# Linear recurrence kernel: one scan over all tiles and both sums, with carry columns, and a new order of the forward loop

## The chip, the cores and the metric

The program runs on one core of a Trainium2 chip. The metric is the device time of one execution in microseconds; before the change it was 7432.79 us (median of 3 runs, 7431.01 to 7443.61).

## The reference, cut to what matters

Two layers on an image tensor of 4 x 192 x 128 x 128 in fp32. The first (channel attention with depthwise convolutions, seven stages of the program) isn't touched by the change. The second is a recurrence in two directions over the 16384 positions of each image, with 192 channels:

```
def step(carry, kv_t):
    p, q, o = carry
    no = jnp.maximum(o, u + kt)
    A = jnp.exp(o - no)
    Bw = jnp.exp(u + kt - no)
    y = (A * p + Bw * vt) / (A * q + Bw)
    no2 = jnp.maximum(w + o, kt)
    A2 = jnp.exp(w + o - no2)
    B2 = jnp.exp(kt - no2)
    return ((A2 * p + B2 * vt, A2 * q + B2, no2), y)
...
x_bi = 0.5 * (x_fwd + x_bwd)
h = jax.nn.sigmoid(r) * x_bi
h = (h - mu) * jax.lax.rsqrt(var + LN_EPS) * ln_g + ln_b
out = jnp.einsum('btc,dc->btd', h, Wo)
```

k, v and r are 192 x 192 projections of the normalised input; mu and var are taken over the channels. The layer's input is added to its output.

## The kernel before, in words

**Stages.** The program is a row of stages that begin and end with a barrier of all engines. The last four are wkv_backward and wkv_forward for images 0 and 1, then again for images 2 and 3. The change touches these two functions and their callers' scratch tensors, nothing else.

**Tiles and chunks.** The 384 channels of two images lie in three tiles of 128 partitions. Positions are cut into 32 chunks of CH = 512. A loop (wkv_steps, line 1231) calls step(n) for n from 0 to 37 on every engine: six steps are written out, then a hardware loop of two steps a round, then six more. In step n an engine works on chunk n, n-1, n-2 or further back, and has(n, lag) leaves out what doesn't exist. There is no scheduler: each engine's work stands in the order in which step lists it, the engines run in order, and semaphores named x_done couple them (a wait for x_done of n-1 waits for chunk n-2, since counts begin at one).

**Backward stage, a chunk.** PE forms k (tile pk) and v (tile pv) by project (lines 1204 to 1210, seven products). v's bias comes from three products of a row of ones with the row vrow (line 1348), which open pv's sums. DVE takes k's maximum (line 1418), ACT forms b = exp(k - max) (bl, line 1369), DVE b v (bvl, line 1442); both are stored to HBM for the forward stage. ACT scales both by a per-channel factor (bf, line 1380; bvf, line 1385), and DVE scans each: three scans of 512 for q (qq, called at line 1473) and three for p (pp). The first column of each scan is the carry, a product of the last chunk's end and a factor (lines 1467 and 1468). Then den = bf eu + q (line 1447) and num = bvf eu + p (line 1455), ACT takes 1/den as exp(-ln den) (lines 1390, 1392), and DVE forms y (yb, line 1432).

**Forward stage, a chunk.** b and b v are read back and scaled (lines 1659, 1664), scanned (line 1800) and made into den and num (lines 1753, 1762) as before. PE forms r (pr); ACT forms exp(-r) (sg, line 1669), DVE clamps it (line 1746), and ACT makes the sigmoid in two more passes (1678, 1680). DVE forms num/den (rc, line 1773), adds the backward y (line 1777) and multiplies by the sigmoid: h (hh, line 1781). The norm over channels needs two averages on PE: of h (pm) and of h squared (pq; ACT's squares are hsq, line 1642), both by average (lines 1598 to 1600). From pm and pq come msq, var (line 1769), lv and rs (lines 1683 to 1689); DVE scales h by rs (hn_done, line 1784). PE then forms the output in po: three products with the identity that bring in the residual xr (line 1620), and project with Wo. ACT writes po to xo (ev_done, line 1695), and SP stores it.

```
if has(n, 2):
    pe.wait_ge(h_done, n - 1)
    average(pm, hh[:, h]).then_inc(mean_done, 1)
if has(n):
    wait(pe, er_done, n)
    project(nc, pr, wr, xt[:, h]).then_inc(r_done, 1)
if has(n, 2):
    pe.wait_ge(hsq_done, n - 1)
    average(pq, hsq).then_inc(st_done, 1)
if has(n, 3):
    for tile in range(3):
        mm(po[:, tile, :], ident[:, :], xr[:, g, tile, :], start=True, stop=False, skip_group_check=True)
    pe.wait_ge(hn_done, n - 2)
    project(nc, po, wo, hh[:, g], begin=False).then_inc(o_done, 1)
```

Of the kernel before, what the change touches and what calls it, by code (L numbers as in the profile page):

```python
# [19 lines left out]
ALU = mybir.AluOpType  # L20
# [1222 lines left out]
def wkv_backward(nc, pair, x1, stat1, wkt, wvt, decay, bonus, b_d, bv_d, y_d, mx_d):  # L1243


    with Stage(nc, f"wb{pair}") as st:
# [6 lines left out]
        vrow = st.sb("vrow", [1, 3, 128])  # L1253
        ones = st.sb("ones", [1, CH])
        xt = st.sb("xt", [128, 2, 3, CH])
        bl = st.sb("bl", [128, 2, 3, CH])
        bvl = st.sb("bvl", [128, 2, 3, CH])
        bf = st.sb("bf", [128, 2, 3, CH])
        bvf = st.sb("bvf", [128, 2, 3, CH])
        qq = st.sb("qq", [128, 2, 3, CH + 1])  # L1260
        pp = st.sb("pp", [128, 2, 3, CH + 1])
        den = st.sb("den", [128, 3, CH])
        num = st.sb("num", [128, 2, 3, CH])
# [15 lines left out]
        bv_stored = [st.sem(f"bv_stored{h}") for h in range(2)]  # L1279
        y_stored = [st.sem(f"y_stored{h}") for h in range(2)]  # L1280
        (k_done, v_done, maxed, m_done, s_max, d_done, b_done, f_done, bf_done, bv_done, bvf_done, carried, q_done,
         scanned, den_done, num_done, ln_done, rc_done, y_done, mx_stored) = map(
            st.sem, ("k_done", "v_done", "maxed", "m_done", "s_max", "d_done", "b_done", "f_done", "bf_done", "bv_done",
                     "bvf_done", "carried", "q_done", "scanned", "den_done", "num_done", "ln_done", "rc_done", "y_done",
                     "mx_stored"))
        block = st.block()

        def chunk(n):
            return NCH - 1 - n

        @block.sync
        def _(sp):
# [7 lines left out]
            def step(n, h, t):  # L1300
# [585 lines left out]
```

## Time and profile before

| | |
|---|---|
| median of 3 runs | 7432.79 us |
| the profiled execution | 7438.61 us |
| its span, first to last instruction | 7435.9 us |
| PE busy | 5760.8 us (77%) |
| DVE busy | 5662.4 us (76%) |
| ACT busy | 2748.5 us (37%) |
| first backward stage, its chunks | from 4816 us on |
| last instruction of DVE in the second forward stage | 7418 us |

PE is TensorE, DVE VectorE, ACT ScalarE, POOL GpSimd, SP the queue that issues most DMAs. Busy time counts an engine's instructions; PEclk or the granted clock is TensorE's clock as a share of full speed. A row of the timeline gives start, duration, engine, line, operation, tiles and how many instructions were merged; brackets hold the idle time before it and what ended it.

### The profile page before, as it was taken

How to read it: one execution, taken by the hardware profiler on the slowest of the kernel's cores; microseconds unless marked ns; L12 is line 12 of the kernel's file. 1: busy time of each engine (PE TensorE's matmuls, PEld its weight loads, DVE VectorE, ACT ScalarE, POOL GpSimd, SP SyncE). 2: the span in 40 equal slices, each digit the busy share in tenths (PEclk: the TensorE clock that was granted, in tenths of full speed). 3: DMA queues.
4: the chain of work that ended last, by engine and by line, in shares of the span. 5: the costliest groups of instructions: out<-in, count | busy, mean ns of one | idle time of the engine just before them, and what ended most of it. 6: DMA issues, size and time to landing. Idle time of an engine off the chain costs nothing. (4 is left out here: it accounts for less than half of the span.)

```text
span 7435.9 us, 82986 instructions
## 1 busy us (share of the span) xinstructions
PE 5760.8 (77%) x25278; PEld 2354.1 (32%) x25278; DVE 5662.4 (76%) x5546; ACT 2748.5 (37%) x3703; POOL 341.1 (5%) x539
## 2 busy tenths in 40 slices
PE   0999997799899566455565777699768879985888
PEld 0333332333333465233332222232222223222222
DVE  6333332799999777888885666599979978997998
ACT  0222221111111466111110000055479974556998
POOL 0110100000000000122220000000000000000000
PEclk9999998899999787777777788787779988787999
DMA  7556554999999997899997999754456644445665
GB/s 292 174 177 198 182 190 152 221 270 274 270 275 277 235 230 179 209 247 255 248 249 181 267 270 267 189 186 183 164 198 230 231 164 170 183 178 182 231 230 181
DMA packets 1209065, 1615.58 MB, mean 217 GB/s; under 512 B 87604, under 2 KB 907509, under 8 KB 1195509
## 3 DMA queue, kind: packets, MB, share of 16 engines
q1 hardware_dynamic: 1067125, 1419.06, 65.6%
q10 hardware_dynamic: 115200, 100.71, 5.1%
q0 software_dynamic: 26624, 94.40, 5.1%
q8 instruction: 57, 0.93, 0.1%
q14 instruction: 59, 0.48, 0.0%
HBM read 1006.55 MB, written 607.33 MB: 217 GB/s over the span
## 5 line engine op out<-in xcount | busy, mean ns | idle before, releaser
L501 PE MATMUL dw_p<-dw_it,dw_tt 128*128 128x512 f32 x2304 | 1027.1, 607 | 177.0 <-DMA dw_it<-u 176.3
L541 DVE SCALAR_TENSOR_TENSOR dw_vo<-dw_vi,dw_wv,dw_vo 128x2048 f32<-128x2048 f32 x384 | 903.1, 2352 | 13.6
L836 PE MATMUL bc_p<-bc_z,bc_wc 128*32 128x256 f32 x9216 | 572.8, 414 | 399.4 <-DVE bc_z L875 399.4
L289 PE MATMUL pw_p<-pw_xh,pw_wlo 128*112 128x512 f32 x1536 | 693.2, 601 | 184.4 <-POOL pw_xh L263 184.4
L875 DVE STREAM_TRANSPOSE bc_z<-bc_xp 128x1536 f32<-128x1536 f32 x256 | 711.8, 2850 | 154.1 <-DMA bc_xp<-d 153.7
L1084 PE MATMUL ap_p<-ap_vt,ap_pw 96*96 96x512 f32 x1024 | 584.3, 736 | 186.5 <-DMA ap_xt<-in_x 184.7
L501 PEld LDWEIGHTS dw_p<-dw_it,dw_tt 128*128 128x128 f32 x2304 | 441.7, 193 | 762.5 <-issue 745.4
L516 ACT ACTIVATE dw_ot<-dw_p 128x512 f32<-128x512 f32 x384 | 206.7, 608 | 997.3 <-DMA d<-dw_ot 703.6
L344 DVE COPY pw_ut<-pw_p 112x512 f32<-112x512 f32 x384 | 247.3, 685 | 379.5 <-PE pw_p L295 377.5
L836 PEld LDWEIGHTS bc_p<-bc_z,bc_wc 128*32 128x32 f32 x9216 | 323.8, 119 | 648.5 <-issue 487.2
L814 ACT ACTIVATE bc_xt<-bc_p 128x256 f32<-128x256 f32 x384 | 147.4, 384 | 874.7 <-PE bc_p L836 874.7
L289 PEld LDWEIGHTS pw_p<-pw_xh,pw_wlo 128*112 128x112 f32 x1536 | 261.8, 177 | 608.2 <-issue 534.1
L658 DVE TENSOR_REDUCE gr_ss<-gr_sq 128x24 f32<-128x3072 f32 x64 | 320.8, 5080 | 127.1 <-ACT gr_sq L642 126.8
L1117 DVE TENSOR_TENSOR ap_xo<-ap_p,ap_tt 96x512 f32<-96x512 f32 x256 | 172.9, 685 | 283.1 <-PE ap_p L1084 166.6
L619 PE MATMUL gr_p<-gr_qk 128*48 128x48 f32 x4096 | 290.5, 337 | 123.1 <-DMA gr_qk<-d 87.8
L1084 PEld LDWEIGHTS ap_p<-ap_vt,ap_pw 96*96 96x96 f32 x1024 | 200.5, 202 | 570.1 <-issue 533.9
L642 ACT ACTIVATE gr_sq<-gr_qk 128x3072 f32<-128x3072 f32 x64 | 319.4, 5061 | 159.0 <-DMA gr_qk<-d 120.2
L295 PE MATMUL pw_p<-pw_xh,pw_whi 64*112 64x512 f32 x1536 | 362.6, 604 | 0.0
L619 PEld LDWEIGHTS gr_p<-gr_qk 128*48 128x48 f32 x4096 | 288.4, 239 | 127.2 <-issue 118.8
L339 DVE COPY pw_ut<-pw_p 16x512 f32<-16x512 f32 x128 | 83.7, 692 | 298.4 <-PE pw_p L295 298.4
L321 ACT ACTIVATE pw_ut<-pw_p 112x512 f32<-112x512 f32 x256 | 138.7, 594 | 423.3 <-PE pw_p L295 423.3
L1167 ACT ACT_TABLE_LOAD x1 | 1.3, 1283 | 767.5 <-issue 767.5
(310 smaller groups left out, 9845.4 us busy)
## 6 DMA issues: line engine op xcount, KB each, us to landing
u<-pw_ut SPq DMA_DIRECT2D x64, 2240.0 KB, 12.6
dw_it<-u SPq DMA_DIRECT2D x192, 512.0 KB, 7.2
d<-dw_ot SPq DMA_DIRECT2D x192, 512.0 KB, 7.3
gr_qk<-d SPq DMA_DIRECT2D x128, 768.0 KB, 9.0
bc_xp<-d SPq DMA_DIRECT2D x256, 288.0 KB, 12.0
bc_xp<-d POOLq DMA_DIRECT2D x256, 288.0 KB, 9.9
gs_xt<-in_x SPq DMA_DIRECT2D x24, 2048.0 KB, 7.2
d<-dw_vo SPq DMA_DIRECT2D x96, 512.0 KB, 7.8
```

The costliest lines, as they stand in the source:

```text
L289: mm(pt[m % NBANK][e][:, :], wlo[:, wm], xh[:, h, 2 * e, cols], start=True, stop=False, skip_group_check=True)
L295: last = mm(pt[m % NBANK][e][:, :], whi[p, wm], xh[p, h, 1, cols], start=False, stop=True, skip_group_check=True)
L344: last = nc.vector.tensor_copy(rows_back(0, h, e, m, q), by_row(pt[m % NBANK][e][:, :]))
L501: mm = nc.tensor.matmul(po[c][:, :].rearrange("p (b w) -> p b w", b=B), tt[:, h, 3 * c + dx, 0:H], it[:, h, B * c:B * (c + 1), dx:dx + W], ...
L516: nc.scalar.activation(ot[:, h, c, :], po[c][:, :], ACT.Copy).then_inc(by_act, 1)
L541: nc.vector.scalar_tensor_tensor(vo[:, h], src, w, vo[:, h], ALU.mult, ALU.add).then_inc(tapped, 1)
L619: mm = nc.tensor.matmul(pg[h][p:p + CPG, :], qk[:, h, 0:CPG, w], qk[:, h, CPG:QK, w], start=w < 2, stop=w >= W - 2, skip_group_check=True)
L642: nc.scalar.activation(sq[:, e % 2, :, :].rearrange("p c w -> p (c w)"), qk[:, h, E * e:E * e + E, :].rearrange("p c w -> p (c w)"), ACT.S ...
L658: nc.vector.tensor_reduce(ss[:, n % 2, E * e:E * e + E], sq[:, e % 2, :, :], AX.X, ALU.add).then_inc(reduced, 1)
L836: mm = nc.tensor.matmul(po[q % NBANK][32 * c4:32 * c4 + 32, :, :], wc[:, c, dx, :, :].rearrange("p j r -> p (j r)"), z[:, h, c, :, dx:dx + ...
L875: last = nc.vector.transpose(z[:, h, :, b % 2, 1 + S * k:1 + S * k + S], xp[:, b % 2, k, :, :].rearrange("p s c -> p c s"))
L1084: mm = nc.tensor.matmul(po[2 * q + m][:, :], pw[:, b, k, m * HALF:(m + 1) * HALF], vt[:, b % 2, k, q * SUB:(q + 1) * SUB], start=k == 0, s ...
```

## The change

- b and b v share one tile (bb), their scaled forms another (fb), with one more column for each tile and sum. The carry is written into that column in one operation, the decay is spread into a tile ewt whose carry columns are 0, and one scan of 6 x 513 = 3078 columns takes the place of six of 512.
- den and num become one tile dn, made by three operations of 2 x 512 columns in place of six of 512. ACT scales b and b v by three operations of 2 x 512 in place of six of 512. b and b v are stored and loaded by one DMA in place of two.
- v's bias is no longer added by PE. It is kept as a column vb (twice the bias) and added where h is formed: the one addition of 1536 columns in the forward stage becomes three of 512 with a scalar operand.
- The order inside step changes, in the forward stage on PE, ACT and DVE: ln and exp of den, the products r and the evictions move by one chunk.

PE, the end of one step and the beginning of the next in the forward loop (wf_po the output, wf_pm and wf_pq the averages of h and of h squared, wf_pr the product r). Before:

```order
L1210 MATMUL wf_po<-wf_hh,wf_wo 64x512
...
L1598 MATMUL wf_pm<-wf_hh,wf_oneb 128x512
L1599 MATMUL wf_pm<-wf_hh,wf_one 64x512
L1600 MATMUL wf_pm<-wf_hh,wf_one 64x512
...
L1204 MATMUL wf_pr<-wf_xt,wf_wr 128x512
...
L1210 MATMUL wf_pr<-wf_xt,wf_wr 64x512
L1598 MATMUL wf_pq<-wf_hsq,wf_oneb 128x512
...
L1620 MATMUL wf_po<-wf_xr,wf_ident 128x512 x3
```

And with the change:

```order
L1586 MATMUL wf_po<-wf_xr,wf_ident 128x512 x3
...
L1572 MATMUL wf_pm<-wf_hh,wf_oneb 128x512
L1573 MATMUL wf_pm<-wf_hh,wf_one 64x512
L1574 MATMUL wf_pm<-wf_hh,wf_one 64x512
L1204 MATMUL wf_po<-wf_hh,wf_wo 128x512
...
L1210 MATMUL wf_po<-wf_hh,wf_wo 64x512
L1572 MATMUL wf_pq<-wf_hsq,wf_oneb 128x512
L1573 MATMUL wf_pq<-wf_hsq,wf_one 64x512
L1574 MATMUL wf_pq<-wf_hsq,wf_one 64x512
...
L1204 MATMUL wf_pr<-wf_xt,wf_wr 128x512
```

Before, r stood right behind pm and ahead of pq, and po ended the step. Now the step runs r, the identity products, pm, po, pq, and the next step's r stands behind pq.

ACT, one step of the same loop. Before:

```order
L1642 ACTIVATE wf_hsq<-wf_hh 128x1536
...
L1648 ACTIVATE wf_fac<-wf_diff 128x6
L1653 ACTIVATE wf_msq<-wf_pm 128x512
L1659 ACTIVATE wf_bf<-wf_bl,wf_fac 128x512 x3
L1664 ACTIVATE wf_bvf<-wf_bvl,wf_fac 128x512 x3
L1669 ACTIVATE wf_sg<-wf_pr,wf_nrb 128x512 x3
L1674 ACTIVATE wf_rc<-wf_den 128x1536
L1676 ACTIVATE wf_rc<-wf_rc 128x1536
L1678 ACTIVATE wf_sg<-wf_sg,wf_onev 128x1536
```

And with the change:

```order
L1617 ACTIVATE wf_rc<-wf_dn 128x1536
L1619 ACTIVATE wf_rc<-wf_rc 128x1536
L1624 ACTIVATE wf_xo<-wf_po,wf_cb 128x512 x3
L1630 ACTIVATE wf_sg<-wf_pr,wf_nrb 128x512 x3
...
L1636 ACTIVATE wf_fac<-wf_diff 128x6
L1642 ACTIVATE wf_fb<-wf_bb,wf_fac 128x2x512 x3
L1647 ACTIVATE wf_lv<-wf_var,wf_eps 128x512
L1650 ACTIVATE wf_rs<-wf_lv 128x512
L1653 ACTIVATE wf_rs<-wf_lv 64x512 x4
L1657 ACTIVATE wf_sg<-wf_sg,wf_onev 128x1536
L1659 ACTIVATE wf_sg<-wf_sg 128x1536
L1663 ACTIVATE wf_hsq<-wf_hh 128x1536
```

Before, the exponential that reads r stood behind the scalings of b and b v; now it stands ahead of the scaling, and the squares, which opened the step, stand near its end.

The diff, cut to its core (mostly the new lines):

```diff
+def spread_decay(nc, dve, ewt, ew, slot, spread):
+
+    for tile in range(3):
+        last = nc.vector.tensor_copy(ewt[:, tile].rearrange("p b t -> p (b t)"), ew[:, tile, :].to_broadcast([128, 2 * CH + 2]))
+    last.then_inc(spread, 1)
+    dve.wait_ge(spread, 1)
+    nc.vector.memset(ewt[:, :, :, slot:slot + 1], 0.0).then_inc(spread, 1)
+    dve.wait_ge(spread, 2)
+
+
+def carry(nc, dve, m, slots, ends, factor, scanned, carried):
+
+    if isinstance(m, int) and m == 0:
+        nc.vector.memset(slots, 0.0).then_inc(carried, 1)
+    else:
+        dve.wait_ge(scanned, m)
+        nc.vector.tensor_tensor(slots, ends, factor.rearrange("p (t a) -> p t a", a=1).to_broadcast([128, 3, 2]),
+                                ALU.mult).then_inc(carried, 1)
+    dve.wait_ge(carried, m + 1)
...
@@ wkv_backward, PE, ACT, DVE
-                for tile in range(3):
-                    mm(pv[:, tile, :], vrow[:, tile, :], ones[:, :], start=True, stop=False, skip_group_check=True)
-                project(nc, pv, wv, xt[:, h], begin=False).then_inc(v_done, 1)
+                project(nc, pv, wv, xt[:, h]).then_inc(v_done, 1)
...
+                    act.wait_ge(bv_done, n + 1)
+                    wait(act, dn_done, n - 1)
                     for tile in range(3):
...
+                        last = nc.scalar.activation(fb[:, h, tile, :, 0:CH], bb[:, h, tile, :, :], ACT.Copy,
+                                                    scale=fac[:, h, 1, tile:tile + 1])
+                    last.then_inc(fb_done, 1)
...
+                if has(n, 1):
+                    dve.wait_ge(f_done, n)
+                    dve.wait_ge(fb_done, n)
+                    carry(nc, dve, n - 1, fb[:, g, :, :, CH], sums[:, :, :, 0], fac[:, g, 0, :], scanned, carried)
+                    wait(dve, dn_done, n - 1)
+                    nc.vector.tensor_tensor_scan(row(sums[:, :, :, :])[:, ::-1], row(ewt[:, :, :, :])[:, ::-1], row(fb[:, g])[:, ::-1],
+                                                 ewt[:, 2, 1, CH:CH + 1], ALU.mult, ALU.add).then_inc(scanned, 1)
                 if has(n, 2):
...
+                    nc.vector.tensor_tensor(yb[:, h], dn[:, :, 1, :], rc[:, :, :], ALU.mult).then_inc(y_done, 1)
...
@@ wkv_forward, PE
+                if has(n, 1):
+                    pe.wait_ge(x_loaded[g], 64 * (t + h))
+                    wait(pe, er_done, n - 1)
+                    project(nc, pr, wr, xt[:, g]).then_inc(r_done, 1)
                 if has(n, 3):
...
                     for tile in range(3):
                         mm(po[:, tile, :], ident[:, :], xr[:, g, tile, :], start=True, stop=False, skip_group_check=True)
+                if has(n, 2):
+                    pe.wait_ge(h_done, n - 1)
+                    wait(pe, msq_done, n - 2)
+                    average(pm, hh[:, h]).then_inc(mean_done, 1)
+                if has(n, 3):
                     pe.wait_ge(hn_done, n - 2)
                     project(nc, po, wo, hh[:, g], begin=False).then_inc(o_done, 1)
+                if has(n, 2):
+                    pe.wait_ge(hsq_done, n - 1)
+                    wait(pe, var_done, n - 2)
+                    average(pq, hsq).then_inc(st_done, 1)
...
@@ wkv_forward, ACT
+                    act.wait_ge(dn_done, n - 1)
...
+                if has(n, 1):
+                    act.wait_ge(r_done, n)
+                    wait(act, h_done, n - 2)
+                    for tile in range(3):
+                        last = nc.scalar.activation(sg[:, g, tile, :], pr[:, tile, :], ACT.Exp, bias=nrb[:, tile:tile + 1], scale=-1.0)
+                    last.then_inc(er_done, 1)
...
@@ wkv_forward, DVE
                 if has(n, 1):
+                    dve.wait_ge(f_done, n)
+                    dve.wait_ge(fb_done, n)
+                    carry(nc, dve, n - 1, fb[:, g, :, :, 0], sums[:, :, :, CH], fac[:, g, 0, :], scanned, carried)
+                    wait(dve, dn_done, n - 1)
+                    nc.vector.tensor_tensor_scan(row(sums[:, :, :, :]), row(ewt[:, :, :, :]), row(fb[:, g]), ewt[:, 0, 0, 0:1],
+                                                 ALU.mult, ALU.add).then_inc(scanned, 1)
+                if has(n, 3):
...
+                    nc.vector.tensor_tensor(var[:, :], pq[:, :], msq[:, :], ALU.subtract).then_inc(var_done, 1)
+                if has(n, 1):
                     dve.wait_ge(er_done, n)
                     nc.vector.tensor_scalar(flat(sg[:, g]), flat(sg[:, g]), 2.0 ** 60, None, ALU.min).then_inc(cl_done, 1)
...
+                if has(n, 2):
+                    dve.wait_ge(rc_done, n - 1)
+                    nc.vector.tensor_tensor(rc[:, :, :], dn[:, :, 1, :], rc[:, :, :], ALU.mult).then_inc(yf_done, 1)
+                    dve.wait_ge(yf_done, n - 1)
+                    dve.wait_ge(y_loaded[h], 16 * t)
+                    for tile in range(3):
+                        last = nc.vector.scalar_tensor_tensor(rc[:, tile, :], rc[:, tile, :], vb[:, tile:tile + 1],
+                                                              yb[:, h, tile, :], ALU.add, ALU.add)
+                    last.then_inc(hs_done, 1)
...
+                    nc.vector.tensor_tensor(flat(hh[:, h]), flat(rc[:, :, :]), flat(sg[:, h]), ALU.mult).then_inc(h_done, 1)
+                if has(n, 3):
+                    dve.wait_ge(rs_done, n - 2)
+                    nc.vector.tensor_tensor(flat(hh[:, g]), flat(hh[:, g]), flat(rs[:, :, :]), ALU.mult).then_inc(hn_done, 1)
+                if has(n, 1):
+                    dve.wait_ge(scanned, n)
                     wait(dve, ln_done, n - 1)
+                    wait(dve, yf_done, n - 1)
                     for tile in range(3):
...
+                        last = nc.vector.scalar_tensor_tensor(dn[:, tile], fb[:, g, tile, :, 1:CH + 1], eu[:, tile, :],
+                                                              sums[:, tile, :, 0:CH], ALU.mult, ALU.add)
+                    last.then_inc(dn_done, 1)
```

## Rows read from the trace of the kernel before

**Rows 1.** Stretches: length, busy PE, PEld, DVE, ACT, POOL, PEclk, DMA share, GB/s

```profile
6800.00:7340.00 540.00, 476.59 (x1214) 148.56 (x1212) 529.57 (x606) 496.49 (x657) 0.00 (x0) 0.92 0.66 226
6200.00:6660.00 460.00, 425.42 (x916) 135.55 (x915) 453.86 (x567) 236.22 (x323) 0.00 (x0) 0.81 0.49 184
```

**Rows 2.** Timeline of DVE, one step of the backward loop (start us, us)

```profile
6300.35 3.64 DVE L1473 TENSOR_TENSOR_SCAN wb_qq<-wb_ew,wb_qq,wb_bf 128x512 f32<-128x512 f32 x3
...
6307.54 3.63 DVE L1473 TENSOR_TENSOR_SCAN wb_pp<-wb_ew,wb_pp,wb_bvf 128x512 f32<-128x512 f32 x3
6311.20 2.08 DVE L1455 SCALAR_TENSOR_TENSOR wb_num<-wb_bvf,wb_eu,wb_pp 128x512 f32<-128x512 f32 x3
...
6317.20 0.16 DVE L1467 TENSOR_TENSOR wb_qq<-wb_qq,wb_fac 128x3 f32<-128x3 f32 x1
...
6317.47 3.64 DVE L1473 TENSOR_TENSOR_SCAN wb_qq<-wb_ew,wb_qq,wb_bf 128x512 f32<-128x512 f32 x3
```

**Rows 3.** Groups of instructions by line: busy us, mean ns of one, idle before

```profile
L1473 DVE TENSOR_TENSOR_SCAN wb_pp<-wb_ew,wb_pp,wb_bvf 128x512 f32<-128x512 f32 x192 | 232.2, 1265 | 0.0
L1455 DVE SCALAR_TENSOR_TENSOR wb_num<-wb_bvf,wb_eu,wb_pp 128x512 f32<-128x512 f32 x192 | 132.9, 747 | 4.7
L1390 ACT ACTIVATE wb_rc<-wb_den 128x1536 f32<-128x1536 f32 x64 | 94.9, 1483 | 23.1 <-DVE wb_den L1447 20.9
```

**Rows 4.** Waits of DVE over the whole execution, and the bias products of a step

```profile
DVE wb_bvl L1442 <- PE wb_pv L1210: 18.5, 4, 6.9
...
6305.69 3.66 PE L1348 MATMUL wb_pv<-wb_ones,wb_vrow 1*128 1x512 f32 x6 [0.68 <-DVE wb_bvl L1442]
```

**Rows 5.** Timeline of DVE and ACT, one step of the forward loop

```profile
6998.89 3.63 DVE L1800 TENSOR_TENSOR_SCAN wf_qq<-wf_ew,wf_qq,wf_bf 128x512 f32<-128x512 f32 x3
...
7004.56 1.84 ACT L1669 ACTIVATE wf_sg<-wf_pr,wf_nrb 128x512 f32<-128x512 f32 x3 [1.42 <-PE wf_pr L1210]
...
7010.81 1.75 DVE L1773 TENSOR_TENSOR wf_rc<-wf_num,wf_rc 128x1536 f32<-128x1536 f32 x1
7012.77 1.76 DVE L1777 TENSOR_TENSOR wf_num<-wf_rc,wf_yb 128x1536 f32<-128x1536 f32 x1 [0.21 <-DVE wf_rc L1773]
7014.56 1.76 DVE L1781 TENSOR_TENSOR wf_hh<-wf_num,wf_sg 128x1536 f32<-128x1536 f32 x1
...
7016.46 1.12 PE L1598 MATMUL wf_pm<-wf_hh,wf_oneb 128*128 128x512 f32 x2 [2.46 <-DVE wf_hh L1781]
...
7018.34 0.95 DVE L1746 TENSOR_SCALAR wf_sg<-wf_sg 128x1536 f32<-128x1536 f32 x1
...
7019.47 1.28 DVE L1800 TENSOR_TENSOR_SCAN wf_qq<-wf_ew,wf_qq,wf_bf 128x512 f32<-128x512 f32 x1
```

**Rows 6.** Timeline of PE in the forward loop: pq, identity, po, and pm

```profile
7066.01 1.13 PE L1598 MATMUL wf_pq<-wf_hsq,wf_oneb 128*128 128x512 f32 x2
...
7068.08 2.84 PE L1620 MATMUL wf_po<-wf_xr,wf_ident 128*128 128x512 f32 x6
7070.76 1.02 PE L1204 MATMUL wf_po<-wf_hh,wf_wo 128*128 128x512 f32 x2
...
7074.97 0.59 PE L1210 MATMUL wf_po<-wf_hh,wf_wo 128*64 128x512 f32 x1
```

**Rows 7.** Timeline of PE after two longer idle times, and TensorE's clock by stretch

```profile
7405.88 2.07 PE L1598 MATMUL wf_pm<-wf_hh,wf_oneb 128*128 128x512 f32 x2 [6.75 <-DVE wf_hh L1781]
...
7409.79 1.25 PE L1598 MATMUL wf_pq<-wf_hsq,wf_oneb 128*128 128x512 f32 x2
...
5468.59 2.07 PE L1598 MATMUL wf_pm<-wf_hh,wf_oneb 128*128 128x512 f32 x2 [8.15 <-DVE wf_hh L1781]
...
5472.50 2.08 PE L1204 MATMUL wf_pr<-wf_xt,wf_wr 128*128 128x512 f32 x2
5474.37 1.20 PE L1205 MATMUL wf_pr<-wf_xt,wf_wr 128*128 128x512 f32 x2
...
7058.60:7062.10 3.50, 3.50 (x7) 1.10 (x7) 3.34 (x9) 3.28 (x6) 0.00 (x0) 0.53 0.86 280
```

More of the change, by code:

```diff
@@ L1445, in step @@
                     wait(dve, ln_done, n - 1)
+                    wait(dve, y_done, n - 1)
                     for tile in range(3):
-                        last = nc.vector.scalar_tensor_tensor(den[:, tile, :], bf[:, g, tile, :], eu[:, tile, :],
-                                                              qq[:, g, tile, 1:CH + 1], ALU.mult, ALU.add)
-                    last.then_inc(den_done, 1)
-                    dve.wait_ge(bvf_done, n)
-                    scans(g, pp, bvf).then_inc(scanned, 1)
@@ L1471, in scans @@
[L1471 to L1476 removed]
+                        last = nc.vector.scalar_tensor_tensor(dn[:, tile], fb[:, g, tile, :, 0:CH], eu[:, tile, :],
+                                                              sums[:, tile, :, 1:CH + 1], ALU.mult, ALU.add)
@@ L1671, in step @@
[L1671 to L1676 removed]
+                        last = nc.scalar.activation(fb[:, h, tile, :, 1:CH + 1], bb[:, h, tile, :, :], ACT.Copy,
+                                                    scale=fac[:, h, 1, tile:tile + 1])
@@ new lines, in step @@
+                    last.then_inc(fb_done, 1)
+                if has(n, 3):
+                    act.wait_ge(var_done, n - 2)
+                    nc.scalar.activation(lv[:, :], var[:, :], ACT.Ln, bias=eps[:, 0:1]).then_inc(lv_done, 1)
+                    act.wait_ge(lv_done, n - 2)
+                    wait(act, hn_done, n - 3)
+                    nc.scalar.activation(rs[:, 1, :], lv[:, :], ACT.Exp, scale=-0.5)
+                    for tile, lo in ((0, 0), (2, 64)):
+                        for p in (0, 64):
+                            last = nc.scalar.activation(rs[p:p + 64, tile, :], lv[lo:lo + 64, :], ACT.Exp, scale=-0.5)
+                    last.then_inc(rs_done, 1)
@@ L1755, in step @@
-                    last.then_inc(den_done, 1)
-                if has(n, 1):
-                    dve.wait_ge(bvf_done, n)
-                    scans(g, pp, bvf).then_inc(scanned, 1)
-                    dve.wait_ge(scanned, n)
-                    wait(dve, hs_done, n - 1)
-                    for tile in range(3):
-                        last = nc.vector.scalar_tensor_tensor(num[:, tile, :], bvf[:, g, tile, :], eu[:, tile, :],
-                                                              pp[:, g, tile, 0:CH], ALU.mult, ALU.add)
-                    last.then_inc(num_done, 1)
@@ L1798, in scans @@
-            def scans(h, sums, term):
-                for tile in range(3):
-                    last = nc.vector.tensor_tensor_scan(sums[:, h, tile, 1:CH + 1], ew[:, tile, :].to_broadcast([128, CH]),
-                                                        term[:, h, tile, :], sums[:, h, tile, 0:1], ALU.mult, ALU.add)
-                return last
+                        last = nc.vector.scalar_tensor_tensor(dn[:, tile], fb[:, g, tile, :, 1:CH + 1], eu[:, tile, :],
+                                                              sums[:, tile, :, 0:CH], ALU.mult, ALU.add)
```

291 lines of the change are left out of this document (83 added, 208 removed).

## The prediction

> **What bounds the kernel now.** The change touches only the last four stages, so I began with the busy time by stretch [rows 1]. In the forward loop DVE is busy for 529.57 of 540 us (98%) and ACT for 496.49 (92%), in the backward loop DVE for 453.86 of 460 (99%) and ACT for 51%. So today both loops go at the pace of DVE, and ACT has 8% to spare in the forward one. Then the timelines: the same scan returns after 17.12 us backward (6300.35 to 6317.47) [rows 2] and after 20.58 us forward (6998.89 to 7019.47) [rows 5]. That is one step, one chunk. There are 32 chunks in each of two backward and two forward stages.
>
> A DVE that is full says only that shorter DVE work may help; whether it does depends on what the new order makes of the loop. So I then followed, engine by engine, what each operation stands behind and what it waits for.
>
> **The change, part by part: DVE's work.** Three scans last 3.63 us and one alone 1.265, so they follow each other by (3.63 - 1.265)/2 = 1.18 us for 512 columns [rows 2, 3]. The trace has only this one length. If nothing of it were fixed, 3078 columns would take 3078/512 x 1.265 = 7.6 us; if a column cost only what it costs the addition of 1536 (1.76 us, so 1.15 ns) [rows 5], 3.5 us. The nearest row for the fixed part is the other three-operand operation, three of which last 2.08 and one 0.747, so 0.67 apart [rows 2, 3]: about 0.12 us fixed. With that a scanned column costs (1.18 - 0.12)/512 = 2.07 ns and the long scan 6.5 us. I take 6.5 and keep 3.5 and 7.6.
>
> By the Trainium skill's page DVE: opcode table, instruction layouts, handler registers and perf-mode slots (section Datapath and trigger behaviour) the scan "runs at half throughput"; that would be 6.4 us as an estimate, and no row here separates it from the fixed part.
>
> Before, a step held 3.54 + 3.66 us of scans (a scan with a waiting successor goes 3.66, 6307.54 to 6311.20 [rows 2]). Now 6.53: saved 0.67. The six operations for den and num took 6 x 0.67 = 4.02; three of 1024 columns take 3 x (2 x 0.67 - 0.12) = 3.66: saved 0.36. Two carry products become one: 0.27 (6317.20 to 6317.47 [rows 2]) becomes 0.19, saved 0.08. **Backward, a step: 1.11 us less**, 17.12 to 16.01. I looked for what could take DVE's place there: ACT's work falls from 51% of a step, PE loses the three bias products (3.66 us a step [rows 4]), and the scan of chunk n-1, which now waits for both scaled tiles, has den and num of the chunk before and the next maximum between them and itself (3.7 + 1.8 us, while ACT's whole work of a step is 236.22/460 x 17.12 = 8.8 us, of which the scaling is a part [rows 1]). So it stays with DVE: 32 x 1.11 = 35.5 us. At its start a backward stage waits for v (18.5 us in 4 waits over both stages [rows 4]); two of these get shorter by the 3.66 us of bias products, 7 us a stage. At its end, ln and exp of the last den (2 x 1.483 us [rows 3]) no longer lie beside a scan: 3 us back. About 39.5 us a stage, **79 us less for both**. The tile ewt I cost at nothing, since DVE fills it while the weights are loaded; without that cover its three copies of 1026 columns would cost some 2 us a stage (the clamp takes 0.95 us for 1536 [rows 5]).
>
> The VectorE page (VectorE: DVE Perf Modes, section on the TRN2 errata) gives a fixed part of only 58 cycles, 0.06 us, for an operation. By it the nine operations fewer would save 0.54 us a step, not 1.11, and the total would be 36 us higher. The rows show about 0.12, and the sum goes by them.
>
> **The forward order.** DVE's own work there falls by 0.67 + 0.36 + 0.08, and the addition with the bias, three operations (2.08) and a wait in place of 1.79 (7012.77 to 7014.56 [rows 5]), gives back 0.34: 19.8 us against 20.58. But PE's and ACT's new orders close a ring. PE now runs r of the next chunk behind pq; pq stands behind po, po behind pm; pm waits for h. h needs DVE's sums, DVE comes to them only after the clamp, and the clamp waits for ACT's exponential of r, in the same step. So every step holds, one behind the other: r; exponential; clamp; num/den; sum; h; pm; po; pq; and then the next r. Before, r stood behind pm, and neither po nor pq lay between h and r; DVE didn't reach h through r of the same step alone.
>
> The ring's price, from start to start: r, seven products like po's, which run from 7070.76 to 7074.97 + 0.59, 4.80 us [rows 6]; exponential 1.84 and two hops of 0.05 [rows 5]; clamp 0.86 (0.95 less an overlap of 0.09); num/den 1.96 (7010.81 to 7012.77); the three additions 2.13; h until pm starts 1.90 (7014.56 to 7016.46) [rows 5]; pm, po, pq. At full clock pm is like pq, 2.07 (7066.01 to 7068.08), and po 4.80 [rows 6]. Sum: 4.80 + 1.94 + 0.86 + 1.96 + 2.13 + 1.90 + 2.07 + 4.80 + 2.07 = **22.5 us**. That is more than the 20.58 of today before anything else is counted.
>
> Then the clock. In the ring PE stands idle from the end of the identity products (2.68 us behind r [rows 6]) to h: 1.94 + 0.86 + 1.96 + 2.13 + 1.90 - 2.68 = 6.1 us, in every step. Today it is idle for 2.46 us there [rows 5], and even so its clock drops to 0.53 for the next 3.5 us, the 1.2 GHz level [rows 7]. After 6.75 us of idle, pm took 3.91 us and what followed ran at full speed but for 0.1; after 8.15 us pm took 3.91, and the next two products 1.87 and 1.04 where they take 0.85 and 0.86, 1.2 us more [rows 7]. So pm costs 1.84 more and po 0.1 to 1.2 more; I take 0.7. **A forward step: 25.1 us**, between 24.5 and 25.6, against 20.58: 4.5 us more. The ring is closed in 30 of a stage's steps (po begins with step 3 and r ends with step 32), and at the end pq of the last chunk stands behind one more po, 5 us: 30 x 4.5 + 5 = 140 us a stage, **280 us more for both**.
>
> The transfers I cost at nothing: b and b v are one DMA of the same bytes, SP waits for nothing later than before, and DMA's share is 0.66 forward and 0.49 backward [rows 1].
>
> **The sum.** 7438.6 (the profiled execution) - 79 + 280 = 7639.6. That execution lies 5.8 us above the median of 7432.8, so I forecast **7634 us** for the median, slower by 2.7%.
>
> **The rivals.**
> (a) The ring isn't closed: some wait is met earlier than I read it and DVE still sets the pace, as its 98% today suggests [rows 1]. Then a forward step takes 19.8, 50 us less for both stages, and with the backward 79 less: 7433 - 129 = 7304 us. For it speaks that ACT already waits for r today (1.42 us [rows 5]) without harm. Against it speaks the order of the rows. It decides at one number: the kernel gets faster only if a forward step stays under 20.58 + (79 - 10)/60 = 21.7 us.
> (b) The ring is closed but PE keeps its full clock: 22.5 us a step, 2 x (30 x 1.9 + 5) = 124 more, 79 less: 7478 us. Against it, each of the idle rows [rows 7]. The page TensorE: Matmul & The Clock Gate (Part 1) says that for modeling the ramp is under 1% of a typical span; the difference between (b) and my forecast is 2.1%, so by that rule (b) would be it.
> (c) The long scan costs 7.6 us. The forward ring hides it, since the scan isn't in it; the backward gain falls by 64 x 1.07 = 68: 7702 us. If it costs 3.5, the backward stages gain 192 more: 7442 us, no change. The fixed parts speak against both.
>
> **How the numbers follow.** About 0.2%, 15 us, is what a measurement can tell from no change. My forecast 0.74, (a) 0.13, (b) 0.07, (c) dear 0.04, (c) cheap 0.02. Slower by more than 0.2%: 0.74 + 0.07 + 0.04 = 0.85, less 0.01 for a ring and clock that both come out short, 0.84; faster: (a) and half of the cheap scan, 0.14; the same 0.02. The range: a step of 24.5 gives 36 us less, and a backward gain larger by 20 another 20 less: 7578. It reaches down towards (b), to 7540, since the clock is the least certain term; upwards a step of 25.6 gives 30 more, with part of the dear scan 7710. Left out are (a), (b) and the cheap scan.
>
> **What would show it.** In the changed profile: a forward loop with DVE busy near 80%, a wait of DVE's clamp on ACT's exponential of r of some 5 us a step, PE idle for about 6 us ahead of pm and pm at half clock in every step, and a step of 25 us. In the backward loop one scan of 3078 columns of 6.6 us, DVE still busy to 98%, a step of 16.0 us. I am wrong if DVE is busy to 95% and more in the forward loop, or if PE shows no idle time ahead of pm.

## The result and the profile after

| | before | after |
|---|---|---|
| median | 7435.3 us (4 runs, 7431.0 to 7443.6) | 7571.5 us (4 runs, 7565.4 to 7575.9) |
| profiled span | 7435.9 us | 7563.8 us |
| PE busy | 77% | 5523.5 us (73%) |
| DVE busy | 76% | 5564.5 us (74%) |

The kernel became slower: the ratio is 1.0174, with a 95% interval of 1.0159 to 1.0188, so about 136 us by the medians. (One execution of e6 below, 8987.6 us at a granted clock of 0.60, was a slow one and isn't in its row.) The forecast was 7634 us, and the range 7540 to 7710. The direction and the mechanism came out as forecast; the size was 201 us in the forecast and 136 in the runs.

The busy time of the changed kernel by stretch (us; then busy time and instructions of PE, PEld, DVE, ACT, POOL; granted clock; DMA share; GB/s), a forward and a backward stretch, to be put beside [rows 1]:

```profile
6880.00:7420.00 540.00, 410.18 (x1016) 122.87 (x1018) 430.60 (x355) 410.20 (x490) 0.00 (x0) 0.85 0.58 194
6280.00:6680.00 400.00, 284.57 (x703) 89.38 (x702) 396.15 (x302) 200.64 (x225) 0.00 (x0) 0.90 0.51 195
```

Backward, DVE is still the bound (99% busy). Forward, it is busy for 430.60 of 540 us, 80%, where it was busy to 98%, and no other engine took its place: PE and ACT are both at 76%. So it is waits between the engines that set the step. The groups say for whom:

```profile
L1720 DVE TENSOR_TENSOR_SCAN wf_sums<-wf_ewt,wf_fb 128x3078 f32<-128x3078 f32 x64 | 424.3, 6630 | 2.3
L1751 DVE SCALAR_TENSOR_TENSOR wf_dn<-wf_fb,wf_eu,wf_sums 128x1024 f32<-128x1024 f32 x192 | 234.9, 1278 | 0.0
L1729 DVE TENSOR_SCALAR wf_sg<-wf_sg 128x1536 f32<-128x1536 f32 x64 | 61.3, 959 | 250.1 <-ACT wf_sg L1630 250.1
L1630 ACT ACTIVATE wf_sg<-wf_pr,wf_nrb 128x512 f32<-128x512 f32 x192 | 118.1, 686 | 300.4 <-PE wf_pr L1210 300.4
L1572 PE MATMUL wf_pm<-wf_hh,wf_oneb 128*128 128x512 f32 x128 | 132.3, 1137 | 384.2 <-DVE wf_hh L1742 384.2
```

The last three rows are the ring: the clamp waits 250.1 us for ACT's exponential, that exponential 300.4 us for r, and pm, over the 64 chunks of both stages, 384.2 us (6.0 a chunk, 5.7 to 5.9 in the steady steps) for h. Before, that wait was 198.7 us in all, and 2.4 to 2.5 a step in the steady part. One step of it in the timeline (start, duration, engine, line, operation, idle time before and its releaser), rows of all three engines:

```profile
7149.82 2.07 PE L1572 MATMUL wf_pm<-wf_hh,wf_oneb 128*128 128x512 f32 x2 [5.74 <-DVE wf_hh L1742]
7153.73 1.57 PE L1204 MATMUL wf_po<-wf_hh,wf_wo 128*128 128x512 f32 x2
7159.01 1.13 PE L1572 MATMUL wf_pq<-wf_hsq,wf_oneb 128*128 128x512 f32 x2
7161.08 1.13 PE L1204 MATMUL wf_pr<-wf_xt,wf_wr 128*128 128x512 f32 x2
7166.04 1.84 ACT L1630 ACTIVATE wf_sg<-wf_pr,wf_nrb 128x512 f32<-128x512 f32 x3 [4.98 <-PE wf_pr L1210]
7167.91 0.96 DVE L1729 TENSOR_SCALAR wf_sg<-wf_sg 128x1536 f32<-128x1536 f32 x1 [4.44 <-ACT wf_sg L1630]
7168.79 1.75 DVE L1732 TENSOR_TENSOR wf_rc<-wf_dn,wf_rc 128x1536 f32<-128x1536 f32 x1
7170.67 2.08 DVE L1736 SCALAR_TENSOR_TENSOR wf_rc<-wf_rc,wf_vb,wf_yb 128x512 f32<-128x512 f32 x3
7172.78 1.76 DVE L1742 TENSOR_TENSOR wf_hh<-wf_rc,wf_sg 128x1536 f32<-128x1536 f32 x1
7174.67 2.07 PE L1572 MATMUL wf_pm<-wf_hh,wf_oneb 128*128 128x512 f32 x2 [5.90 <-DVE wf_hh L1742]
7178.57 1.13 PE L1204 MATMUL wf_po<-wf_hh,wf_wo 128*128 128x512 f32 x2
```

Each row is the first of a group that starts when the group above it is done (pm has six products, po and r fourteen): 24.85 us from pm to pm. pm takes 3.91 us both times (7149.82 to 7153.73), and the granted clock in it is 0.50, the 1.2 GHz level; from 7160 to 7165, with PE busy throughout, it is 1.00:

```profile
7149.80:7153.50 3.70, 3.68 (x6) 0.79 (x6) 3.15 (x3) 3.64 (x4) 0.00 (x0) 0.50 0.62 219
7160.00:7165.00 5.00, 5.00 (x17) 1.65 (x18) 3.48 (x2) 1.06 (x2) 0.00 (x0) 1.00 0.82 256
```

The backward step, answering to [rows 2], is one scan and 15.86 us from scan to scan (the steps alternate between 15.85 and 15.95, where they were 17.1):

```profile
6354.27 6.63 DVE L1436 TENSOR_TENSOR_SCAN wb_sums<-wb_ewt,wb_fb 128x3078 f32<-128x3078 f32 x1
...
6370.13 6.63 DVE L1436 TENSOR_TENSOR_SCAN wb_sums<-wb_ewt,wb_fb 128x3078 f32<-128x3078 f32 x1
```

**The account.** From the first to the last start of the operation that forms h, a forward stage takes 745.2 us both times (the second from 6786.23 to 7531.39) where it took 636.4 and 635.7: 108.8 and 109.5 more, 218 for both. From the first to the last negated maximum, a backward stage takes 484.7 where it took 528.1 and 526.3: 43.4 and 41.6 less, 85 for both. The remaining parts at the ends of the stages add some 6. These four stages together are 139 us longer. The stages ahead of them, which the change doesn't touch, were 11 us shorter in this execution (the first loop starts 4811.7 us into the span with after and 4824.7 with before; the other 2 us of this difference lie in the first backward stage's own start and are counted in the 139; such starts lay between 4799 and 4843 in the runs below). 139 - 11 = 128 is the difference of the spans. Because the untouched part wanders like this, the experiments below are compared by step lengths as well as by times.

### The profile page after: what moved, and what is told of

Its sections match the earlier page's. It is cut to its first block and busy times, and to the rows that moved or that the text cites. A ratio compares the mean times of both kernels' runs of the same rounds, so it can differ in the third digit from the quotient of the medians.

```text
span 7563.8 us, 80038 instructions
## 1 busy us (share of the span) xinstructions
PE 5523.5 (73%) x24890; PEld 2270.0 (30%) x24890; DVE 5564.5 (74%) x4534; ACT 2683.1 (35%) x3319; POOL 342.1 (5%) x539
## 5 line engine op out<-in xcount | busy, mean ns | idle before, releaser
L1436 DVE TENSOR_TENSOR_SCAN wb_sums<-wb_ewt,wb_fb 128x3078 f32<-128x3078 f32 x64 | 424.3, 6630 | 2.3
L1720 DVE TENSOR_TENSOR_SCAN wf_sums<-wf_ewt,wf_fb 128x3078 f32<-128x3078 f32 x64 | 424.3, 6630 | 2.3
L1572 PE MATMUL wf_pm<-wf_hh,wf_oneb 128*128 128x512 f32 x128 | 132.3, 1137 | 384.2 <-DVE wf_hh L1742 384.2
L1389 ACT ACTIVATE wb_fb<-wb_bb,wb_fac 128x1024 f32<-128x1024 f32 x192 | 206.7, 1140 | 475.9 <-DVE wb_bb L1445 475.9
```

The costliest lines, as they stand in the source:

```text
L1436: nc.vector.tensor_tensor_scan(row(sums[:, :, :, :])[:, ::-1], row(ewt[:, :, :, :])[:, ::-1], row(fb[:, g])[:, ::-1], ewt[:, 2, 1, CH:CH + ...
L1720: nc.vector.tensor_tensor_scan(row(sums[:, :, :, :]), row(ewt[:, :, :, :]), row(fb[:, g]), ewt[:, 0, 0, 0:1], ALU.mult, ALU.add).then_inc( ...
```

## The experiments

Unless said otherwise each edit is made on the changed kernel ("after"). The step is the mean distance of h from h in the steady part of the second forward stage. All ratios are to before, with runs of before on the same chip.

| run | ratio to before [95%] | median us | forward step | backward step |
|---|---|---|---|---|
| before | 1 | 7435.3 | 20.5 | 17.1 |
| after | 1.0174 [1.0159, 1.0188] | 7571.5 | 24.4 | 15.9 |
| e1_r_ahead | 0.9800 [0.9784, 0.9817] | 7277.1 | 19.5 | 15.9 |
| e2_pq_behind_r | 1.0154 [1.0137, 1.0171] | 7545.2 | 23.9 | 15.9 |
| e3_filler | 1.0051 [1.0030, 1.0071] | 7469.0 | 22.7 | 15.9 |
| e7_pq_filler | 0.9925 [0.9908, 0.9942] | 7379.6 | 21.3 | 15.9 |
| e4_six_scans | 0.9889 [0.9871, 0.9907] | 7360.7 | 20.0 | 16.4 |
| e5_six_scans_late_r | 1.0223 [1.0202, 1.0245] | 7608.8 | 24.4 | 16.4 |
| e8_order_before | 1.0565 [1.0540, 1.0590] | 7858.4 | 29.0 | 15.9 |
| e10_er_first | 1.0176 [1.0153, 1.0198] | 7561.3 | 23.9 | 15.9 |
| e6_bias_backward (3 runs) | 0.9775 [0.9748, 0.9801] | 7284.6 | 19.3 | 15.9 |

**Is it a ring? (e1_r_ahead)** PE forms r a step earlier, and nothing else changes:

```diff
-                if has(n, 1):
-                    pe.wait_ge(x_loaded[g], 64 * (t + h))
-                    wait(pe, er_done, n - 1)
-                    project(nc, pr, wr, xt[:, g]).then_inc(r_done, 1)
+                if has(n):
+                    pe.wait_ge(x_loaded[h], 64 * (t + 1))
+                    wait(pe, er_done, n)
+                    project(nc, pr, wr, xt[:, h]).then_inc(r_done, 1)
```

> One edit to the changed kernel: in the forward stage PE forms r of chunk n in step n again (before, the change had moved it to chunk n-1), so that ACT's exponential of r finds it ready and r is no longer a link between pq and h. Ring theory: the forward step falls from 24.4 us to DVE's own work, 19.8 us, DVE's wait of the clamp on ACT (250 us over the execution) goes, PE's idle time ahead of pm falls below 3 us; 60 steps x 4.6 us less: about 7290 us, faster than before the change too. Rival (what the forward stage lost is due to the longer work itself, the three additions with the bias and the later var, not to the order of r): the step stays above 22 us and the time above 7430 us.

Measured: 0.9800 of before, step 19.5 us, 294 us under after. The same loop in its timeline and by stretch:

```profile
7001.27 0.95 DVE L1729 TENSOR_SCALAR wf_sg<-wf_sg 128x1536 f32<-128x1536 f32 x1
7007.85 1.12 PE L1572 MATMUL wf_pm<-wf_hh,wf_oneb 128*128 128x512 f32 x2
```

```profile
6700.00:7200.00 500.00, 438.91 (x1175) 138.65 (x1174) 492.56 (x411) 468.86 (x563) 0.00 (x0) 0.96 0.69 239
```

Neither the clamp nor pm has idle time before it any more, pm's first two products take 1.12 us instead of 2.07, and DVE is busy to 99%. One place on PE decided between 7277 and 7572, and with it the changed kernel is faster than the one before.

**How much of the ring is the clock? (e3_filler)** Five products whose result nobody reads go into the wait ahead of pm:

```diff
                 if has(n, 2):
-                    pe.wait_ge(h_done, n - 1)
                     wait(pe, msq_done, n - 2)
+                    for k in range(5):
+                        mm(pm[:, :], oneb[:, :], wr[:, 0:CH], start=True, stop=True, skip_group_check=True)
+                    pe.wait_ge(h_done, n - 1)
                     average(pm, hh[:, h]).then_inc(mean_done, 1)
```

> Work added to the changed kernel and nothing removed: in the forward stage PE runs five more products of 128x512 with constant operands into pm (about 4.3 us) in the idle time ahead of h, overwritten by pm's own. Theory that the half clock behind the idle time is a part of the ring: pm falls from 3.9 us to about 2.1 and the first product of po to its full speed, the step falls by 1.9 us to 22.5 us: about 7455 us, although PE does more. Rival (the clock costs nothing on the path): the time stays at 7571 us; rival (the filler itself delays pm): slower than 7571 us.

```profile
7154.18 1.13 PE L1572 MATMUL wf_pm<-wf_hh,wf_oneb 128*128 128x512 f32 x2 [1.54 <-DVE wf_hh L1744]
7156.43 1.13 PE L1204 MATMUL wf_po<-wf_hh,wf_wo 128*128 128x512 f32 x2
```

```profile
6900.00:7300.00 400.00, 370.16 (x988) 124.10 (x987) 343.97 (x286) 327.33 (x390) 0.00 (x0) 1.00 0.61 208
```

The clock stays at 1.00, pm takes 2.25 us with its last wait (7154.18 to 7156.43) instead of 3.91, the step is 22.67 against the 22.5 worked out for full clock, and the kernel is 102 us faster by the medians for doing more work (91 by the ratios to before; the two forward stages are 105 us shorter from first to last h). So the ring has two parts: about 22.5 us of work behind one another, and 1.9 of lowered clock.

**A shorter ring (e2_pq_behind_r), and the same at full clock (e7_pq_filler).** The second average moves from behind po to behind r; e7 has the filler products of e3 as well:

```diff
+                if has(n, 3):
+                    pe.wait_ge(hsq_done, n - 2)
+                    wait(pe, var_done, n - 3)
+                    average(pq, hsq).then_inc(st_done, 1)
                 if has(n, 3):
                     pe.wait_ge(r_loaded[g], 64 * (t + h - 1))
...
-                if has(n, 2):
-                    pe.wait_ge(hsq_done, n - 1)
-                    wait(pe, var_done, n - 2)
-                    average(pq, hsq).then_inc(st_done, 1)
```

> One edit to the changed kernel: the average of the squares (pq) of chunk n-3 stands behind r of chunk n-1 in the same step instead of ahead of it. Ring theory: pq (2.07 us) leaves the link between po and r, but r now reaches the clamp through pq and var (2.7 us) instead of the exponential (1.94 us), so the ring gets 1.3 us shorter: a step of 23.1 us, about 7490 us. Rival (PE's order is not what binds): no change, 7571 us. Rival (the ring gives back all of pq): 2.07 us a step, 7447 us.

> e2_pq_behind_r (the second average behind r) with the five filler products of e3_filler ahead of the mean; nothing is left out. It asks what ate most of the gain that e2_pq_behind_r was to bring. Theory A (the clock: the step of e2 lost its gain because the stretch of products at half clock got longer): at full clock the shorter ring shows whole, the step is 1.1 to 1.3 us under the 22.67 of e3_filler, so 21.4 to 21.6, and the time about 75 us under e3_filler, near 7395. Theory B (the new wait of VectorE for the second average's variance is the bound in itself): the step stays within 0.4 us of e3_filler's, 22.3 or more, time 7445 or more.

e2 missed its number: 23.9 us a step, 0.5 less than after, where 1.3 was expected. Its timeline shows why (pm, then the first and second pair of po):

```profile
7159.14 2.07 PE L1572 MATMUL wf_pm<-wf_hh,wf_oneb 128*128 128x512 f32 x2 [4.71 <-DVE wf_hh L1742]
...
7163.05 1.88 PE L1204 MATMUL wf_po<-wf_hh,wf_wo 128*128 128x512 f32 x2
7164.76 1.02 PE L1205 MATMUL wf_po<-wf_hh,wf_wo 128*128 128x512 f32 x2
```

po's first pair takes 1.71 us here (7163.05 to 7164.76), and 1.71 and 1.78 in turn over the steps, where at full clock it takes 0.96: pm and po together lose 2.6 us to the clock in each step here, and 2.0 in the mean of after. In e7, at full clock, the same move is worth 1.4 us (22.67 to 21.27), and the time is 7379.6. So the ring did get shorter by about what it should, and 0.6 us of the gain went to the clock (2.6 - 2.0). Most of the 0.3 us that are left lies in e3, whose po waits 0.1 and 0.2 us in turn, in the second case for DVE's product with rs (from pm to po it takes 2.25 and 2.34 us there, against 2.07), which it does not in after. Theory B of e7, a bound in the new wait for the variance, falls.

**What is the merge of the scans worth, and where? (e4_six_scans, e5_six_scans_late_r)** The same edit on e1 and on after:

```diff
-                    nc.vector.tensor_tensor_scan(row(sums[:, :, :, :]), row(ewt[:, :, :, :]), row(fb[:, g]), ewt[:, 0, 0, 0:1],
-                                                 ALU.mult, ALU.add).then_inc(scanned, 1)
+                    for tile in range(3):
+                        for part in range(2):
+                            last = nc.vector.tensor_tensor_scan(sums[:, tile, part, :], ewt[:, tile, part, :],
+                                                                fb[:, g, tile, part, :], ewt[:, 0, 0, 0:1],
+                                                                ALU.mult, ALU.add)
+                    last.then_inc(scanned, 1)
```

> Like e1_r_ahead, but the one scan over 3078 columns is cut into six over 513 columns each (every sum of every tile, each from its own zero decay column), in both stages. Nothing else changes. This prices the merge of the scans by itself, on a kernel in which VectorE is the bound in both stages. Theory (the step of the prediction that took 6.5 us for one scan against the six of before, 1265 ns each behind one another at about 1.2 us): six of 513 columns give a sixth part of 6.63 us each, plus about 0.12 us for each boundary between them, so five boundaries, 0.6 us per step, in 128 steps: +80 us against e1_r_ahead, near 7355. Rival (a fixed part of some 0.06 us per instruction, which the pages state): +0.3 us per step, +40 us, near 7315. Rival (scans behind one another without a dependence overlap): nothing, 7277.

> The changed kernel, order and all, with its one scan over 3078 columns cut into six over 513 in both stages, the same edit that e4_six_scans made on the kernel with r ahead. There it cost 0.55 us per step backward and 0.35 to 0.43 forward. Theory (the forward stage is a ring through PE, ScalarE and VectorE, and the scan lies in front of VectorE's wait for the clamp, outside it): the forward step stays at its 24.3 us mean, the wait ahead of the clamp shrinks from 4.4 by about 0.5, and only the backward stages pay, 16.4 us each: +33 us against the changed kernel, near 7604. Rival (VectorE's own work still counts in the forward stage, since a longer scan pushes the whole step back): +60 us or more, 7632.

With DVE as the bound (e4), six scans last 7.17 us where the one lasts 6.63:

```profile
6313.09 7.17 DVE L1438 TENSOR_TENSOR_SCAN wb_sums<-wb_ewt,wb_fb 128x513 f32<-128x513 f32 x6
```

That is 0.54 us a backward step (15.90 to 16.44), 0.11 per boundary; a forward step gets 0.45 longer (in the mean over both stages), and the time came out at 7360.7, where 7355 was expected. In the ring (e5) the backward step grows by the same 0.54 and the forward step not at all: 743.9 us from first to last h where after has 745.2. The time, 7608.8, is within 5 us of the 7604 that the backward stages alone give. What grows is DVE's work ahead of the clamp, at the expense of its wait, 250.1 us in after and 215.0 here:

```profile
DVE wf_sg L1737 <- ACT wf_sg L1634: 215.0, 60, 5.0
```

So in the changed kernel the long scan of the forward stages gained nothing: what it saved, DVE spent waiting at the clamp.

**Does only r's place matter? (e8_order_before, e10_er_first)** Here TensorE's whole forward order is the one of before, while DVE and ACT keep theirs; e10 exchanges two groups on ACT as well:

```diff
+                if has(n, 2):
...
+                    average(pm, hh[:, h]).then_inc(mean_done, 1)
+                if has(n):
...
+                    project(nc, pr, wr, xt[:, h]).then_inc(r_done, 1)
+                if has(n, 2):
...
+                    average(pq, hsq).then_inc(st_done, 1)
                 if has(n, 3):
...
                     project(nc, po, wo, hh[:, g], begin=False).then_inc(o_done, 1)
```

and on ACT, in e10 alone:

```diff
-                if has(n, 4):
...
-                    last.then_inc(ev_done, 1)
                 if has(n, 1):
                     act.wait_ge(r_done, n)
...
                     last.then_inc(er_done, 1)
+                if has(n, 4):
...
+                    last.then_inc(ev_done, 1)
```

> The changed kernel with TensorE's forward order exactly as in the kernel before (mean of n-2, r of n, second average of n-2, residual and output projection of n-3), while VectorE and ScalarE keep the changed order and the merged operations. Theory (only the place of r matters; the rest of TensorE's order is slack): the same time as e1_r_ahead, within 15 us, forward step near 19.5, near 7277. Rival (the second average now stands ahead of the output projection and holds it until ScalarE's squares come, last in its step, and the next h waits for the projection that reads its slot): forward step 20.5 or more, 7340 or more.

> e8_order_before with two groups of ScalarE's forward step exchanged: the exponentials of r for n-1 now stand ahead of the eviction of the output projection, where they stood behind it. e8_order_before took 28.6 to 29.5 us per step, and its trace shows ScalarE 10 us idle at that eviction, since the projection now comes last on TensorE, with the exponentials queued behind the waiting eviction and the clamp, h and the next mean behind those. Theory (that queue place closes a second ring, through the projection and the eviction): with the exponentials first the ring is open, VectorE's 19.4 to 19.6 us per step are the bound again, ratio to before near 0.98, 7280 to 7300. Rival (the late second average or the projection's slot holds the step in another way): step still over 21 us, 7380 or more.

Both theories of mine were refuted. The times fell on the side of the two rivals (7340 or more, 7380 or more), but the waits aren't the ones that the first of them named. e8 takes 28.6 and 29.5 us a step in turn. ACT in e8, then ACT and DVE in e10:

```profile
7330.09 1.84 ACT L1623 ACTIVATE wf_xo<-wf_po,wf_cb 128x512 f32<-128x512 f32 x3 [9.29 <-PE wf_po L1210]
7331.82 1.85 ACT L1629 ACTIVATE wf_sg<-wf_pr,wf_nrb 128x512 f32<-128x512 f32 x3
```

```profile
7214.60 1.84 ACT L1629 ACTIVATE wf_xo<-wf_po,wf_cb 128x512 f32<-128x512 f32 x3 [4.90 <-PE wf_po L1210]
7216.33 0.21 ACT L1635 ACTIVATE wf_fac<-wf_diff 128x6 f32<-128x6 f32 x1
7216.62 3.23 ACT L1641 ACTIVATE wf_fb<-wf_bb,wf_fac 128x1024 f32<-128x1024 f32 x3
```

```profile
7223.59 1.76 DVE L1744 TENSOR_TENSOR wf_hh<-wf_hh,wf_rs 128x1536 f32<-128x1536 f32 x1 [4.54 <-ACT wf_rs L1652]
```

In e8 the exponential of r has its operand long ago, but stands in ACT's queue behind the eviction of po, which waits 9.29 us for a projection that now comes last on PE. That is a second ring: pm, r, pq, identity products, po, eviction, exponential, clamp, h. In e10 the exponential is ahead, and the step falls from 29.0 to 23.9, which shows that the second ring was the bound of e8. By the trace a third ring takes over, further down the same queue (no run opens this one, so it is read and not tested): behind the waiting eviction (4.90 us) stand fb and rs, DVE's product with rs waits 4.54 us for rs, and den and num, the scan and the next h stand behind that. From this eviction (7214.60) over that h to the pm behind it (7243.39) are 28.8 us, and from the pm before (7195.60) over r, pq, identity products and po to the eviction are 19.0: 47.8 us, which is two steps of 23.9. ACT's order in the changed kernel needs po early on PE. So the changed order of PE is not a mistake as a whole: of the orders run here with ACT's new one, it is the fastest once r stands a step ahead.

**The bias (e6_bias_backward, on e1_r_ahead).** In the backward stage ACT adds v's bias to y in place, and the forward sum is one addition again:

```diff
+                if has(n, 2):
+                    act.wait_ge(y_done, n - 1)
+                    for tile in range(3):
+                        last = nc.scalar.activation(yb[:, h, tile, :], yb[:, h, tile, :], ACT.Identity, bias=vb[:, tile:tile + 1])
+                    last.then_inc(yv_done, 1)
...
+                    nc.vector.tensor_tensor(flat(rc[:, :, :]), flat(rc[:, :, :]), flat(yb[:, h]), ALU.add).then_inc(hs_done, 1)
```

> Like e1_r_ahead, but v's bias is added to the stored y in the backward stage, by three in-place operations on ScalarE (which stands idle there half the time) between fac and fb of a step, and the forward stage forms the sum in one addition over 1536 columns again; the bias no longer goes through memory. Theory (the prediction's term of 0.34 us per step for the bias additions; ScalarE's three operations fit beside VectorE's product for b v, which fb waits for anyway): -0.34 x 64 = -22 us against e1_r_ahead, near 7255, VectorE's forward step 19.2 in place of 19.5, the backward step unchanged at 15.9. Rival (fb comes later by the three operations, and the next scan waits for it): backward step up by 1 us or more, +40 us or more in all, slower than e1_r_ahead.

The backward step stayed at 15.9, and the forward stages became 5.6 and 7.6 us shorter instead of 11 each. Since that run and e1's were on different chips, both were run again on one:

> e1_r_ahead word for word, run on the chip on which e9_bias_backward_again runs, to have both against one set of runs of before. Expected 0.98 of before, as on the first chip.

> e6_bias_backward word for word on the same chip as e9_r_ahead_again. Its forward stages were 5.6 and 7.6 us shorter from first to last h than those of e1_r_ahead, its backward stages equal, while stages that both share differed by 30 us between the two chips. Expected: 13 to 20 us under e9_r_ahead_again. If it is not under it by at least 5 us, the bias in the backward stage gives nothing.

Measured: 7289.3 us (0.9797, 0.9777 to 0.9817) for e1's kernel and 7282.4 us (0.9787, 0.9764 to 0.9809) for the one with the bias moved. The forward stages are again 7 to 8 us shorter each, 594.2 against 602.0 and 601.2, but the medians differ by 7 us and the intervals overlap. The steps show the gain and the whole time can't tell it from nothing.

## Why the prediction was right, and where its size was off

- **The ring** was the step that carried the forecast, and the rows and e1 bear it out: 22.5 us of work without the clock, measured 22.7 in e3; PE idle for 6.1 us ahead of pm, measured 5.7 to 5.9 in the steady steps; DVE 80% busy, measured 80%; the clamp's wait of some 5 us, measured 4.2 in the mean of 60 waits.
- **The clock's term was mis-sized.** I took 1.84 us for pm and 0.7 for po and got 25.1 us a step; the mean is 24.4 without a stage's first and last step. The step lengths run through a pattern of six: 25.53, 24.78, 24.31, 24.18, 23.98 and 23.99 us. Against 2.07 and 4.84 at full clock, pm and po together lose 3.06, 2.28, 1.84, 1.68, 1.51 and 1.50 us in these (worked out from the starts of the groups on PE in six steps), 2.0 in the mean, where I had 2.54. The step that loses 3.06, and one that loses 1.51 (pm, po and the pq behind it):

```profile
7124.36 2.07 PE L1572 MATMUL wf_pm<-wf_hh,wf_oneb 128*128 128x512 f32 x2 [5.91 <-DVE wf_hh L1742]
7128.26 2.08 PE L1204 MATMUL wf_po<-wf_hh,wf_wo 128*128 128x512 f32 x2
7134.33 1.13 PE L1572 MATMUL wf_pq<-wf_hsq,wf_oneb 128*128 128x512 f32 x2
...
7223.15 2.07 PE L1572 MATMUL wf_pm<-wf_hh,wf_oneb 128*128 128x512 f32 x2 [5.91 <-DVE wf_hh L1742]
7226.73 1.12 PE L1204 MATMUL wf_po<-wf_hh,wf_wo 128*128 128x512 f32 x2
7231.57 1.12 PE L1572 MATMUL wf_pq<-wf_hsq,wf_oneb 128*128 128x512 f32 x2
```

  The rows that I read [rows 7] gave 3.91 for pm each time; a pm of 3.57 to 3.76 was not among them, and half of the steps have one. From two steps seen I took the higher end for a quantity that varies from step to step. The step's 0.66 less (25.07 in the sum, 24.41 measured) are 0.66 x 60 = 40 us of the miss, some 34 of them the clock's; the rest is small differences in the other links.
- **The ends of the forward stages.** I counted 30 full steps and 5 us for one more po ahead of the last pq. Only 29 steps of a stage are longer, the last one is even shorter (17 us, before 20), and what follows the last h is hardly longer than before. What the parts ahead of the first h and between the stages took more offsets 6 us of this, and 16 us of the miss are left.
- **The backward gain** was forecast at 39.5 us a stage and measured at 42.5 from the first to the last negated maximum, 6 us of the miss: a step of 15.9 where I had 16.01. The long scan was taken as 6.5 us and measured 6.63, but it overlaps its successor by 0.08 (6354.27 to 6360.82 is 6.55), so 6.55 is what a step pays, about what the sum had. Most of the step's 0.11 us less is in the three operations for den and num, 3.58 us from start to start (6364.14 to 6367.72) where I had 3.66. The saving at a boundary between scans, taken as 0.12 from the addition's rows, came out as 0.11 in e4.
- **Rival (a)**, 7304 us if the ring were open, is what e1 built: 7277, at a step of 19.5 where (a) had 19.8. **Rival (b)**, 7478 at full clock, is e3: 7469. The page TensorE: Matmul & The Clock Gate (Part 1) of the Trainium skill lets one leave the ramp out as under 1% of a span; here the 102 us between after and e3 are 1.4% of the whole, and by it the forward step would have been 22.5 instead of 24.4.
- **Rival (c)** fell with the scan's 6.63 us, between 3.5 and 7.6.
- **The fixed part of an operation.** e4 shows 0.11 us for each scan more, close to the 0.12 that the sum went by. The Trainium skill's 58 cycles (VectorE: DVE Perf Modes, section on the TRN2 errata) would be 0.06; the runs don't agree with it here. My prediction left out that the same section calls this row too low, and gives 151 cycles, 0.16 us, for the duration of a single fp32 tensor_tensor; what one more operation cost in e4 lies between the two.

40, 16 and 6 are the 62 us between the 201 forecast and the 139 by which the four stages grew; the medians say 136.

What stays open: why the step lengths of after repeat over six steps, and whether e10 would reach DVE's pace with its third ring opened; neither was tried.

## What to carry to other kernels

Before merging operations on the engine that is full, follow each engine's queue in the new order and add up every closed path from an operation back to itself one step later, queue places included (one that comes back two steps later, as in e10, counts half); where the longest of them is longer than the fullest engine's own work, it is the step, and what lies outside it, like the long scan here, gains nothing. Where two orders are to be exchanged, exchange them on all engines together or test each place: PE's old order under ACT's new one was worse (29.0 us a step) than either. Where TensorE stands idle in such a ring, add what its lowered clock costs behind the gap, from several steps of a trace rather than from one or two.

## What the runs showed of the hardware

- Work that nobody needs made the kernel faster: 5 products more in each of the 64 forward steps, 102 us less, granted clock 1.00 in the loop instead of 0.85.
- A gap of 4.5 to 4.7 us ahead of pm (e2) cost more clock, 2.6 us, than one of 5.7 to 5.9 us (after), 1.5 to 3.1 us with a mean of 2.0. The length of the gap alone doesn't set the loss. And a short gap has one too: before, with 2.4 to 2.5 us ahead of pm, pm and the r behind it took 1.6 us longer than the 2.07 and 4.84 at full clock in each steady step, where DVE, busy to 98%, set the pace:

```profile
7160.11 1.33 PE L1598 MATMUL wf_pm<-wf_hh,wf_oneb 128*128 128x512 f32 x2 [2.44 <-DVE wf_hh L1781]
7163.28 1.63 PE L1204 MATMUL wf_pr<-wf_xt,wf_wr 128*128 128x512 f32 x2
7168.62 1.13 PE L1598 MATMUL wf_pq<-wf_hsq,wf_oneb 128*128 128x512 f32 x2
```

- Stage lengths were the same to 0.5% on different chips and in different executions (the backward loop with the one scan 484.6 to 484.8 us in every run, whatever else was changed forward; the forward loop of e1's kernel 602.6 and 602.5 us on one chip, 602.0 and 601.2 on another; of e6's 597.0 and 594.9, then 594.3 and 594.2), while the stages ahead of them moved by up to 44 us between runs.
